# Three buffers for the rows scaled by B, and one copy of the turned dt u, in the two state-space layers

## The reference

```
u  = silu(conv(x_in) + conv_b)            # 4 taps along the tokens
dt = softplus(dt_r @ W_dt + b_dt)         # dt_r, B, C = split(u @ W_xp)
h[t] = h[t-1] * exp(dt[t] * A) + (dt[t] * u[t]) * B[t]
y[t] = sum over the 16 states of h[t] * C[t]
out = x + gate * ((y + u * D) * silu(z)) @ W_out
```

## Time and profile before

| | |
|---|---|
| median of the runs | 3047.9 us |
| the profiled execution, own time | 3052.71 us |
| its span | 3051.0 us |
| granted TensorE clock, mean | 0.930 |
| layer 1, first and last start of a POOL product | 386.4 and 1273.1 us |
| layer 3, the same | 2099.9 and 3008.7 us |

### The profile page before, as it was taken

The page is one execution under the profiler, slowest core; times in us unless marked ns, Lnnn a source line. Parts: engine busy times, 40 slices in busy tenths (PEclk is TensorE's granted clock), DMA queues, the critical chain, the costliest instruction groups (busy, mean ns, idle before and its releaser), DMA issues. The chain is left out here.

```text
span 3051.0 us, 44181 instructions
## 1 busy us (share of the span) xinstructions
PE 2470.3 (81%) x14532; PEld 1683.7 (55%) x14532; DVE 2178.6 (71%) x2878; ACT 2160.8 (71%) x3593; POOL 1690.6 (55%) x1365
## 2 busy tenths in 40 slices
PE   7778578888889888736899998857888888888885
PEld 4555257667667677612333333324667666676674
DVE  4443388788788788656777776616889889888883
ACT  2333499988989889613666665537989879889993
POOL 0000078878878889650111111015879889889895
PEclk9999799999999999867999999879999999999997
DMA  3000201112011111046554544011112112112121
GB/s 114 28 27 21 81 29 58 46 49 66 36 58 65 36 51 58 30 86 89 78 85 85 83 79 78 15 60 49 37 57 72 43 66 65 57 51 72 56 65 44
DMA packets 106124, 177.01 MB, mean 58 GB/s; under 512 B 10709, under 2 KB 91405, under 8 KB 97199
## 3 DMA queue, kind: packets, MB, share of 16 engines
q1 hardware_dynamic: 101679, 161.69, 20.6%
q0 software_dynamic: 4224, 12.59, 1.3%
HBM read 139.70 MB, written 34.14 MB: 57 GB/s over the span
## 5 line engine op out<-in xcount | busy, mean ns | idle before, releaser
L1105 POOL TENSOR_TENSOR l_h<-l_h,l_c_all 128x512 f32<-128x512 f32 x1024 | 1382.0, 1368 | 262.3 <-DVE l_h L1022 246.1
L1022 DVE TENSOR_TENSOR_SCAN l_h<-l_dA,l_ps_dbu 128x512 f32<-128x512 f32 x1024 | 1224.1, 1211 | 283.0 <-ACT l_dA L895 163.3
L877 ACT ACTIVATE l_dub<-l_duT,l_b_tok 128x512 f32<-128x512 f32 x1024 | 731.2, 715 | 164.0 <-PE l_ps_dbu L1284 163.3
L1284 PE MATMUL l_ps_dbu<-ident,l_dub 128*128 128x128 f32 x4096 | 637.7, 279 | 173.3 <-ACT l_dub L877 103.0
L895 ACT ACTIVATE l_dA<-l_dt,l_a_neg 128x512 f32<-128x512 f32 x1024 | 730.9, 714 | 5.0 <-issue 4.8
L1269 PE MATMUL l_ps_y<-ident,l_h 128*128 128x128 f32 x4096 | 631.0, 278 | 13.7 <-POOL l_h L1105 12.7
L1284 PEld LDWEIGHTS l_ps_dbu<-ident,l_dub 128*128 128x128 f32 x4096 | 477.7, 143 | 228.7 <-DVE l_h L1022 115.8
L1269 PEld LDWEIGHTS l_ps_y<-ident,l_h 128*128 128x128 f32 x4096 | 491.8, 144 | 133.1 <-issue 86.5
L1779 ACT ACTIVATE l_probs<-l_ring 128x512 f32<-128x512 f32 x512 | 293.0, 598 | 269.8 <-PE l_ring L1917 268.6
L1598 DVE TENSOR_REDUCE l_q_max<-l_ring 128x1 f32<-128x512 f32 x512 | 338.6, 683 | 182.3 <-PE l_ring L1910 178.4
L1917 PE MATMUL l_ring<-l_qs,l_ks 102*128 102x512 bf16 x512 | 203.3, 401 | 57.1 <-DMA l_qs<-l_m_parts 44.7
(11 more groups left out here) (248 smaller groups left out, 2946.5 us busy)
## 6 DMA issues: line engine op xcount, KB each, us to landing
l_c_all<-c_rows_dram SPq DMA_DIRECT2D x64, 1024.0 KB, 4.8
l_res<-x_dram SPq DMA_DIRECT2D x24, 512.0 KB, 6.5
parts_dram<-l_parts SPq DMA_DIRECT2D x48, 256.0 KB, 2.8
l_qs<-parts_dram SPq DMA_DIRECT2D x48, 256.0 KB
l_ks<-parts_dram SPq DMA_DIRECT2D x48, 256.0 KB
l_x_in<-x_dram SPq DMA_DIRECT2D x16, 512.0 KB, 7.2
x_dram<-l_res SPq DMA_DIRECT2D x16, 512.0 KB, 3.1
l_x_in<-in_x SPq DMA_DIRECT2D x8, 512.0 KB, 4.2
```

The source lines that it names most:

```text
L877: return act.activation(dub[:, n % 2, t, :], duT[:, p, t, :], ACT.Copy, scale=b_tok[:, p, t, n:n + 1])
L1022: dve.tensor_tensor_scan(h[:, h_slot(s), :], dA[:, s % DA_RING, :], ps_dbu[:, dbu_slot(s), :], 0.0, ALU.mult, ALU.add).then_inc(scan_ok, 1)
L1105: pool.tensor_tensor(h[:, h_slot(s), :], h[:, h_slot(s), :], c_all[:, (n // C_GROUP) % 2, n % C_GROUP, :], ALU.mult).then_inc(hc_ok, 1)
L1284: last = pe.transpose(ps_dbu[:, dbu_slot(s), t * P:(t + 1) * P], dub[:, n % 2, t, j * P:(j + 1) * P], ident[:])
```

## The change

`dub` gets three slots in place of two, and `duT` one copy in place of two (the two tiles together keep their size). A table says which slot a row has: rows 0 to 14 take slots 0, 1, 2 in turn, row 15 takes slot 1. `dub_back(n)` is the number of rows back to the last one in row n's slot: 2 for rows 1 and 15, 4 for rows 0 and 2, and 3 for all others. ACT's wait ahead of a row is set by it: with a distance of 3 it may begin row n + 1 at unit 4n when the transposes of row n - 2 are done, the last of which is that of unit 4n - 5. For rows 1 and 15 the wait is as before.

With a single `duT`, `du_tok` of the next batch overwrites what this batch's row 15 still reads. So it waits for that row's quarter (a new semaphore, `row_ok`, for quarters 0 to 2, and `dub_ok` for the last), and both sides of this wait are on ACT. Row 15 is made at units 56 to 59.

```diff
+DUB_SLOTS = tuple(n % 3 for n in range(N - 1)) + (1,)
+
+def dub_back(n):
+    return next(d for d in range(1, N + 1) if DUB_SLOTS[(n - d) % N] == DUB_SLOTS[n])
...
-        duT = sb("duT", [P, 2, TB, DI])
+        duT = sb("duT", [P, TB, DI])
...
-        dub = sb("dub", [P, 2, TB, DI])
+        dub = sb("dub", [P, 3, TB, DI])
...
-                def du_tok(b, p, t):
+                def du_tok(b, t):
                     act.wait_ge(duT_tr, b * TB + t + 1)
-                    act.activation(duT[:, p, t, :], bank(b, "du", t), ACT.Copy).then_inc(duT_ok, 1)
+                    if first(b):
+                        pass
+                    elif t < TB - 1:
+                        act.wait_ge(row_ok, b * (TB - 1) - (TB - 1) + t + 1)
+                    else:
+                        act.wait_ge(dub_ok, b * N)
+                    act.activation(duT[:, t, :], bank(b, "du", t), ACT.Copy).then_inc(duT_ok, 1)
...
                 def scale_rows(p, n, t):
-                    return act.activation(dub[:, n % 2, t, :], duT[:, p, t, :], ACT.Copy, scale=b_tok[:, p, t, n:n + 1])
+                    return act.activation(dub[:, DUB_SLOTS[n], t, :], duT[:, t, :], ACT.Copy, scale=b_tok[:, p, t, n:n + 1])
...
                         if not first(b):
-                            act.wait_ge(dbu_ok, b * UNITS - JB + CREDIT)
+                            act.wait_ge(dbu_ok, b * UNITS - (dub_back(0) - 1) * JB + CREDIT)
...
                             if j == 0:
-                                act.wait_ge(dbu_ok, b * UNITS + n * JB + CREDIT)
+                                act.wait_ge(dbu_ok, b * UNITS + (n + 2 - dub_back(n + 1)) * JB + CREDIT)
                             last = scale_rows(p, n + 1, j)
                             if j == TB - 1:
                                 last.then_inc(dub_ok, 1)
+                            elif n + 1 == N - 1:
+                                last.then_inc(row_ok, 1)
...
-                            last = pe.transpose(ps_dbu[:, dbu_slot(s), t * P:(t + 1) * P], dub[:, n % 2, t, j * P:(j + 1) * P], ident[:])
+                            last = pe.transpose(ps_dbu[:, dbu_slot(s), t * P:(t + 1) * P], dub[:, DUB_SLOTS[n], t, j * P:(j + 1) * P], ident[:])
```

More of the change, by code:

```diff
@@ L667, in mamba @@
             sem("y"), sem("out_mm"), sem("og"), sem("res_ld"), sem("res"), sem("stored"), sem("y_st"), sem("yr_ld"))
-        gate_ld, prep_v, ln_step, dt_exp, a_ok, dtr_ok, shift_ok, diag_ok, st_ok = (
-            sem("gate_ld"), sem("prep_v"), sem("ln_step"), sem("dt_exp"), sem("a_ok"), sem("dtr"), sem("shift"), sem("diag_d"), sem("st"))
+        gate_ld, prep_v, ln_step, dt_exp, a_ok, dtr_ok, shift_ok, diag_ok, st_ok, row_ok = (
+            sem("gate_ld"), sem("prep_v"), sem("ln_step"), sem("dt_exp"), sem("a_ok"), sem("dtr"), sem("shift"), sem("diag_d"), sem("st"), sem("row"))
         def rows_of(ap, b):
@@ L868, in prep_step @@
                     elif s in (45, 47, 49, 51): z_part(b, p, (s - 45) // 2)
-                    if s in (57, 59, 61, 63): du_tok(b, p, (s - 57) // 2)
+                    if s in (57, 59, 61, 63): du_tok(b, (s - 57) // 2)
                 def far_step(s, b):
```

## The result

The changed kernel took 2971.05 us, the median of four runs (2963.35 to 2972.66), against 3046.28 us of the kernel before (four runs, 3041.17 to 3048.7). The ratio is 0.9744 with a 95% interval of 0.9727 to 0.9761: faster. The forecast was 2963 us within 2944 to 2990; the measured time is 8 us above it, and the gain is 75 us in place of 85. A second series of the same kernel gave 2966.69 us, ratio 0.9724 (0.9706 to 0.9743). The profiled execution took 2969.68 us with a span of 2968.0 and a granted clock of 0.936 (before 0.930).

A forecast was written before the change was run, and what follows sets the result against it. PE and DVE were taken to pace units 0 to 28 and ACT units 29 to 63. Terms 28.5 + 46.9 + 3.8 + 6.0 = 85.2 us off 3047.9 gave 2963 us, range 2944 to 2990.

The forecast's parts named there:

- The half that each engine paces, and the wait at unit 28: PE and DVE pace units 0 to 28, ACT units 29 to 63; loosening ACT's unit 28 wait starts `silu_u` earlier.
- rival 4: No change: the waits' numbers bind elsewhere or PE bounds the second half too; 3048 us, chance 0.05.
- The waits at 12 and 24 worth nothing for themselves: ACT's waits at units 12 and 24 count nothing themselves, but their removal carries ACT to unit 28 early.
- The hand-over of 0.1 us from tap to `silu_u`: At unit 28, `silu_u` waits for DVE's last tap alone and follows it by 0.1 us, table load already done.
- short-kind: Five of bodies 1 to 6 in both layers, like body 3 of layer 1: 5.7 us each, 28.5 us.
- long-kind: Seven of bodies 1 to 6 in both layers, like body 2 of layer 1: 6.7 us each, 46.9 us.
- Unit 33: ACT's copy of PE's x projection, ready about 663.1 not 662.4, cuts 7.4 us to 6.7 in seven bodies.
- One `duT` at nothing: 56 copies at units 57 to 63 wait for ACT's own quarters; taken as nothing, upper bound 40 us.
- Rival 3: Slower: copies' waits at units 57 to 63 cost more than they hide; 3075 us at 2.0 us each, chance 0.04.
- rival 1: Only scan 29's holes close, ACT's lead is lost in units 29 to 63: 66 us gain, 2982 us, chance 0.18.
- rival 2: Layer 3's long softplus step on DVE costs six bodies 5.2 us: 31 us back, 2994 us, chance 0.10.
- Next late is the last tap, and a fourth slot would add nothing: At unit 28 DVE's last tap is late next, behind it DVE's first half; a fourth slot adds nothing.

## Why the prediction was right, and by how much off

*The half that each engine paces, and the wait at unit 28.* Shown by the two kernels that split the waits: this one alone gives 72.5 of 77.9 us in the layers, all the others without it nothing. So the mechanism was right. "PE bounds it all" (rival 4) is out: PE was busy for 81% of the span and is for 82%, and 75 us went without touching its work. The prediction misread the rule of the Trainium skill ("Perfetto Trace Analysis", "Identifying the Most-Contended Engine") where it put PE first with 81%. That section says that for TensorE the busy share of matmuls is not a good measure of how close one is to the limit, and asks for the share of the weight loads instead, which is 55% before the change. By that measure DVE and ACT stand first with 71% each, so the rule would not have passed ACT over. Taken by stretch the rows decide: in the second half ACT is busy for 58.49 of 61.00 us.

*The waits at 12 and 24 worth nothing for themselves.* Right: a ratio of 1.0005 without the one at 28, and 5.4 us in the layers beside it.

*The hand-over of 0.1 us from tap to `silu_u`.* This is the term that was mis-sized. It is 0.03 to 0.04 us in bodies 0, 5 and 6, and 1.39 or 1.40 in the eight loop bodies, where the table load stands behind the wait. I had put the load among what "is done while DVE still works on the taps", without looking which instruction carries the wait. By the prediction's own working a short-kind loop body then gets 5.82 - 1.40 = 4.4 us in place of 5.7 and a long-kind one 7.5 - 1.4 = 6.1 in place of 6.7 (the wait for the x projection is then not met): three of the one and five of the other, 6.9 us less. Measured in bodies 1 to 4 of both layers: 42.3 us, against 43.7 by this and 50.6 by the forecast. The kernel with the load ahead of the wait is the check: 51.5 us there.

*Unit 33.* The wait for PE's x projection is absent in the loop bodies, 1.9 us in three times (1.1 the longest) in the written-out ones, and 15.2 us once `silu_u` was early; in the version with the load ahead it was at most 0.4 us where the prediction had 0.7. So the prediction was right that the wait appears, and put it too high.

*Bodies 5 and 6*: 22.9 us against 24.8. Body 6 of layer 3 gave 3.5 in place of 5.7; its softplus step on DVE took 7.0 us there, before 5.9, which is half of the difference; the rest is open. *Body 0*: 4.1 against 3.8. *Body 7*: 4.7 and 3.8 us against 3.0 each; with unit 28 alone it was 3.4 and 3.2, so about 1.9 of these 2.5 us come from the other waits, which I had priced at nothing. Sum: 85.2 - 6.9 - 1.4 - 1.9 + 0.3 + 2.5 = 77.8 us. These small terms are as large as the difference between two executions (body 6 of layer 1 took 104.4 us in one trace of the changed kernel and 106.3 in the other), so only the 6.9 us are a finding. That the sum met the layers' 77.9 us and the runs' 75 us so closely is in part luck.

*One `duT` at nothing.* Shown by the kernel that has it alone. Rival 3 fell with it.

*Only the holes close (rival 1, 66 us)* could not be told from the forecast by the time alone: 75 us lies midway between 66 and 85. The loop bodies gained 4.4 to 6.4 us where DVE's longest hole in this half was 4.8. The kernel with the load ahead decides it: 51.5 us in the eight loop bodies, where the holes alone would give 8 x 4.7 = 38. ACT's lead was not lost. *Layer 3 gives back (rival 2)* fell: the long softplus step is in bodies 1 to 6 as before,

```profile
L1000 DVE SCALAR_TENSOR_TENSOR l_dt<-l_conv_in,l_work x64: 659/754/6986, 368.4 to 2814.6; 128x512 f32<-128x512 f32 x64
```

and layer 3 gained 37.0 us all the same. The traces also show what the step waits for: POOL's multiplications. The longest one (over at 2805.48 + 6.99 = 2812.47 us) ends 0.56 us after a stretch in which POOL multiplied without a break, from 2803.26 to 2811.91. All twelve steps above 4.9 us, six in each of the two traces, end 0.55 to 0.56 us after the end of such a stretch. In the changed kernel such a step was held in layer 1 too, where POOL issues no indirect DMA. Body 5, DVE and POOL:

```profile
1003.75 2.67 DVE L1000 SCALAR_TENSOR_TENSOR l_dt<-l_conv_in,l_work 128x512 f32<-128x512 f32 x1
```

```profile
1000.91 4.96 POOL L1121 TENSOR_TENSOR l_h<-l_h,l_c_all 128x512 f32<-128x512 f32 x4
```

The step ends at 1006.42, POOL's stretch at 1005.87. Two taps in each of bodies 0 to 5 of layer 3 are held in the same way, 2.3 to 2.9 us long, before and after; no scan took over 1.3 us. This fits the contention between GpSimd and VectorE instructions with two inputs in SBUF that the Trainium skill names ("GPSIMD Engine Reference", "1. Specifications"), except that four of the twelve taps are first taps, which read one large tile and not two. And the prediction's reading, that the stall goes where such a step meets the DMAs, is too narrow, and no run shows why a step sometimes lets several multiplications pass and at other times gets in between two of them.

*Next late is the last tap, and a fourth slot would add nothing.* The first half of this is shown by ACT's 25.0 + 15.9 us of waits for it. A fourth slot was not tried, nor three slots with two copies of `duT`. But the conclusion that the place was exhausted was wrong: with the tap as the releaser, the order of ACT's own block is worth 18 us in the layers (1720.1 to 1701.9), which the load and `silu_z` ahead of the wait brought in.

## What to carry to other kernels

When a change removes a wait, look at what the next wait will stand in front of: an instruction that was free behind an old event (here a table load) is paid for as soon as its neighbour's event comes last, and work without that dependence belongs ahead of the wait. Sum up an engine's idle time by the place at which it can be felt: of 163 us of waits at the rows one wait per body counted, taking away the others moved them into it, and later 9 us of waits at another place did not shorten the kernel. A time that falls between forecast and rival decides nothing: here a further kernel, which removed the mis-sized term, did. A buffer given up pays for one won where the new wait is for the engine's own older result.

## What the runs showed of the hardware

A wait of ACT for a result of its own, finished 1.1 us before, left no gap (the copy at 697.29, whose quarter was over at 696.19), and the 56 waits of this kind, this one among the shortest, didn't change the time (ratio 0.9994). A table load took 1.28 us, and it begins only when the wait ahead of it is over: 0.11 us after the tap's end, about the 0.12 us with which `silu_u` followed the tap in the loop once the load was ahead; in the written-out bodies, with the wait on the instruction itself, it was 0.03. A DVE step with two inputs in SBUF, 0.7 us at its shortest, took up to 7.0 us while POOL multiplied without a break, and ended 0.56 us after the last multiplication of that stretch. The clock is not behind the gain: the mean granted clock was 0.930 before, 0.936 after, and 0.931 in the kernel with unit 28 alone, whose layers were 72.5 us shorter too.
